# A fused state-space and channel-mix layer: another order in the first and last stages, and products on TensorE that nothing reads

## The reference

```python
def ssm(x):                                   # on the layer norm of x_in, per sequence
    x, z = split(x @ W_in)                    # 256 | 256
    dt, B, C = split(x @ W_x)                 # 256 | 16 | 16
    delta = softplus(dt @ W_dt + b_dt)
    dA = exp(delta * A)                       # 256 x 16 states per token
    h = dA * h_before + (delta * x) * B       # along the 2048 tokens
    y = sum over the 16 states of h * C  + x * D_param
    res = (y * silu(z)) @ W_out + its input
    return layernorm(res) * ln_g + ln_b
x = x_in + ssm(layernorm(x_in))
def ffn(x):                                   # on the layer norm of x
    xr, xk = mixes of x and the token before it (mu_r, mu_k)
    return sigmoid(xr @ W_r.T) * (relu(xk @ W_k.T)**2 @ W_v.T)
out = x + ffn(layernorm(x))
```

## Time and profile before

| | us |
|---|---|
| median of 3 runs | 1011.47 |
| lowest and highest | 1010.65, 1012.99 |
| the profiled execution's own time | 1010.73 |
| its span, from first to last instruction | 1008.9 |
| busy: GpSimd, PE, DVE, ACT | 931.1, 927.5, 918.1, 913.4 |
| mean granted TensorE clock | 0.978 |

### The profile page before, as it was taken

One profiled execution on the slowest core, in us unless ns is written; L12 is line 12 of the kernel. 1 busy time (PEld: TensorE's weight loads), 2 busy tenths in 40 slices (PEclk: granted clock), 3 DMA queues, 4 the chain that ended last, 5 costly groups with the idle time before them and its releaser, 6 DMA issues.

```text
span 1008.9 us, 15660 instructions
## 1 busy us (share of the span) xinstructions
PE 927.5 (92%) x4988; PEld 717.8 (71%) x4988; DVE 918.1 (91%) x1004; ACT 913.4 (91%) x2151; POOL 931.1 (92%) x408
## 2 busy tenths in 40 slices
PE   6658779999999999999999999999999999999996
PEld 3336567777778677777868777786877778688784
DVE  2989999999999999999999999999999999998974
ACT  5787999999999999999999999999999999987854
POOL 0899999999999999999999999999999999999940
PEclk9779999999999999999999999999999999999998
DMA  6444454354535544553655455365445536453410
GB/s 195 175 141 165 180 209 182 144 200 171 194 143 210 208 172 166 181 186 140 211 207 175 162 191 183 134 214 204 172 166 190 194 123 221 176 188 129 155 44 21
DMA packets 51184, 171.97 MB, mean 170 GB/s; under 512 B 5408, under 2 KB 32032, under 8 KB 34720
## 3 DMA queue, kind: packets, MB, share of 16 engines
q1 hardware_dynamic: 51104, 170.99, 46.9%
HBM read 153.67 MB, written 9.44 MB: 162 GB/s over the span
## 4 chain that ended last, share of the span: by engine, by line
ACT 55%; PE 29%; DVE 7%; issue 5%; POOL 2%; DMA 0%; ACTq 0%; SPq 0%; DVEq 0%; POOLq 0%
ACT da_ps L602 17%; PE w_ps L1181 10%; PE w_ps L1188 8%; ACT h_tok L558 3%; DVE hg L947 3%; ACT h_tok L544 3%; PE y_ps L1172 3%; ACT xn_tok L544 3%; PE w_ps L1251 2%; ACT nr L571 2%; PE w_ps L1206 2%; ACT spare L550 2%; ACT xres L782 2%; ACT L746 2%; ACT L737 2%
## 5 line engine op out<-in xcount | busy, mean ns | idle before, releaser
L494 POOL TENSOR_TENSOR dbx<-u,b_ring 128x1024 f32<-128x1024 f32 x255 | 600.3, 2375 | 9.1 <-DVE u L988 8.2
L602 ACT ACTIVATE da_ps<-delta,a_neg 128x512 f32<-128x512 f32 x512 | 332.6, 682 | 23.1 <-DVE hg L947 13.9
L507 POOL TENSOR_TENSOR hg<-hg,c_ring 128x1024 f32<-128x1024 f32 x143 | 340.2, 2379 | 3.8 <-DVE hg L947 3.1
L947 DVE TENSOR_TENSOR_SCAN hg<-da_ps,carry,dbx 128x512 f32<-128x512 f32 x216 | 263.0, 1266 | 11.5 <-ACT da_ps L602 11.4
L1172 PE MATMUL y_ps<-ident,hg 128*128 128x128 f32 x2048 | 260.5, 276 | 9.5 <-POOL hg L507 7.3
L1172 PEld LDWEIGHTS y_ps<-ident,hg 128*128 128x128 f32 x2048 | 238.0, 143 | 38.7 <-issue 21.1
L947 DVE TENSOR_TENSOR_SCAN da_ps<-da_ps,carry,dbx 128x512 f32<-128x512 f32 x168 | 208.6, 1276 | 4.4 <-ACT da_ps L602 4.0
L954 DVE TENSOR_TENSOR hg<-da_ps,c_ring 128x1024 f32<-128x1024 f32 x112 | 137.2, 1225 | 12.2 <-DVE da_ps L947 0.5
L947 DVE TENSOR_TENSOR_SCAN hg<-da_ps,dbx 128x512 f32<-128x512 f32 x72 | 83.8, 1207 | 4.5 <-ACT da_ps L602 4.5
L947 DVE TENSOR_TENSOR_SCAN da_ps<-da_ps,dbx 128x512 f32<-128x512 f32 x56 | 66.6, 1216 | 6.6 <-ACT da_ps L602 5.5
L1181 PE MATMUL w_ps<-xT,w_dtx 128*128 128x512 f32 x120 | 60.0, 623 | 7.2 <-ACT zs L617 6.4
(11 more groups left out here) (199 smaller groups left out, 1502.5 us busy)
## 6 DMA issues: line engine op xcount, KB each, us to landing
b_ring<-bc_rows_dram SPq DMA_DIRECT2D x64, 1024.0 KB, 6.6
c_ring<-bc_rows_dram SPq DMA_DIRECT2D x64, 1024.0 KB, 4.9
xres<-in_L_attn_x_in_dram SPq DMA_DIRECT2D x16, 512.0 KB, 4.7
x_tok<-in_L_attn_x_in_dram SPq DMA_DIRECT2D x15, 512.0 KB, 5.9
res<-xn_tok SPq DMA_DIRECT2D x15, 512.0 KB, 6.7
out_dram<-r_out SPq DMA_DIRECT2D x15, 512.0 KB, 3.2
bc_rows_dram<-bc_rows SPq DMA_DIRECT2D x16, 64.0 KB, 1.6
x_tok<-in_L_attn_x_in_dram SPq DMA_DIRECT2D x2, 256.0 KB, 4.1
```

The lines of the kernel that those rows point to most:

```text
L494: pool.tensor_tensor(dbx[:, n % X_RING, :, :], u[:, ip, :, :], b.to_broadcast([P, KH, LC]), ALU.mult).then_inc(s["dbx_done"], 1)
L507: pool.tensor_tensor(part, part, c_of(n).to_broadcast([P, KH, LC]), ALU.mult).then_inc(s["g_pool"], 1)
L602: act.activation(da_of(n, h), delta[:, ip, h, :], ACT.Exp, scale=a_neg[:, h, n:n + 1]).then_inc(s["da_ready"], 1)
L947: dve.tensor_tensor_scan(out, da_of(n, h), dbx[:, n % X_RING, h, :], 0.0 if first else carry[:, n, h:h + 1], ALU.mult, ALU.add).then_inc(s ...
```

## The change

The column split gets a form in which each chunk may have its own (`SPLITS`, `LAST_SPLIT`). Chunks 0 to 14 keep the old one. In chunk 15, column 12 is multiplied by C on GpSimd and no longer on DVE. The tables of step -1 and step 15 and the bank table of step 15 are all new; of them two lines are shown. The middle's tables stay. The close is reordered on PE, ACT, DVE and GpSimd; the last output half goes out as two blocks of 128 tokens, each with its own store; its second block's v product goes to a bank of its own. `keep_busy` issues products of the identity with part of w_in into a work bank; no engine reads them: four before step 0, two before the turn of h's first half and one after it.

```diff
-SPLIT = [3, 5, 6, 8, 11, 12, 14]
+SPLITS = [[3, 5, 6, 8, 11, 12, 14], [3, 5, 6, 8, 11, 12, 14]]
+LAST_SPLIT = [3, 5, 6, 8, 11, 14]
...
-VEC_HEAD = dict(small=4, sp0=4, sp1=6, u0=7, u1=9, center=11, ffn=13)
+VEC_HEAD = dict(small=6, center=6, ffn=9, sp0=10, sp1=12, u0=12, u1=15)
...
-VEC_TAIL = dict(mix0=0, mix1=0, gate=2, x20=6, x21=6, v0=8, v1=8, late_mix0=10, late_mix1=10, late_v0=14, late_v1=14)
+VEC_TAIL = dict(mix0=1, mix1=1, gate=3, x20=6, x21=6, v0=7, v1=8, late_mix0=9, late_mix1=9, late_v0=14, late_v1=14)
...
+        def split_of(i):
+            return LAST_SPLIT if i == LAST else SPLITS[i % 2]
...
             def close():
-                for v in range(2):
-                    sp.wait_ge(last_out[v], 1)
-                    sp.dma_start(out_v[LAST][:, 2 * v:2 * v + 2, :], r_out[:, 2 * v:2 * v + 2, :]).then_inc(s["out_stored"], 16)
+                sp.wait_ge(last_out[0], 1)
+                sp.dma_start(out_v[LAST][:, 0:2, :], r_out[:, 0:2, :]).then_inc(s["out_stored"], 16)
+                for j in range(2):
+                    sp.wait_ge(last_out[1], j + 1)
+                    sp.dma_start(out_v[LAST][:, 2 + j, :], r_out[:, 2 + j, :]).then_inc(s["out_stored"], 16)
...
             def close():
 
+                pool.wait_ge(s["xres_loaded"], 16 * NT)
+                part = xres[:, LAST % 2, :, :]
+                pool.tensor_tensor(part, part, b_all[:, :].unsqueeze(1).to_broadcast([P, TB, D]), ALU.add).then_inc(s["xb_done"], 1)
                 pool.wait_ge(c_loaded[GROUPS - 1], 16 * NT)
                 pool.wait_ge(s["scan_done"], KH * NS * NT - 1)
                 part = hg[:, (NS - 1) % H_RING, 0:1, :]
                 pool.tensor_tensor(part, part, c_of(NS - 1), ALU.mult).then_inc(s["g_pool"], 1)
-                pool.wait_ge(s["xres_loaded"], 16 * NT)
-                part = xres[:, LAST % 2, :, :]
-                pool.tensor_tensor(part, part, b_all[:, :].unsqueeze(1).to_broadcast([P, TB, D]), ALU.add).then_inc(s["xb_done"], 1)
...
-                    act.wait_ge(s["start_read"], read_before(NS - 1))
+                    act.wait_ge(s["start_read"], read_before(NS - 1 + h))
...
                 norm3(0)
+                share(0, xk, omk, 0)
                 norm3(1)
-                share(0)
-                share(1)
+                share(0, xr, omr, 1)
                 act.wait_ge(s["w_r_turned"], 1)
                 act.activation(w_r_last, w_r_bank, ACT.Copy).then_inc(s["w_r_set"], 1)
                 relu(0)
+                share(1, xk, omk, 0)
+                share(1, xr, omr, 1)
                 act.wait_ge(s["out_stored"], 16 * (NT - 1))
                 tanh(0)
...
                 gate(1)
+                affine_last(0)
                 second(0)
                 mean_of(0)
+                affine_last(1)
+                norm(0)
                 second(1)
-                norm(0)
                 mean_of(1)
+                mix(0, xk, muk, 1)
                 norm(1)
-                mix(0)
-                mix(1)
-                out_of(0)
-                out_of(1)
+                mix(0, h_of, mur, 2)
+                mix(1, xk, muk, 1)
+                mix(1, h_of, mur, 2)
+                out_of(0, by_block(V_LAST[0]), slice(0, 2), 1)
+                out_of(1, v_block(1, 0), 2, 1)
+                out_of(1, v_block(1, 1), 3, 2)
...
+            def keep_busy(bank, n):
+
+                for _ in range(n):
+                    pe.matmul(bank[:, :], ident[:, :], w_in[:, 0, :], start=True, stop=True)
...
                 if t == 0:
                     pe.wait_ge(s["start_read"], len(PRE))
                     pe.wait_ge(s["ffn_ev"], 3)
+                    keep_busy(work[0], 4)
...
-                need(pe, s["g_vec"], len(SPLIT) * NT)
+                pe.wait_ge(s["scan_done"], KH * (NS * NT - 1))
+                need(pe, s["g_vec"], splits(LAST, NS - 1))
                 residual(0)
                 add_up(LAST, NS - 1)
                 gated_turned(0)
                 gated_turned(1)
                 need_all_read(pe, LAST, list(TAIL_BANK))
+                wo(0)
                 residual(1)
-                wo(0)
                 wo(1)
-                h_turned(0)
                 pe.wait_ge(s["w_r_loaded"], 16)
...
                 last.then_inc(s["w_r_turned"], 1)
+                keep_busy(work[1], 2)
+                h_turned(0)
+                keep_busy(work[1], 1)
+                k_of(0)
                 h_turned(1)
-                k_of(0)
-                k_of(1)
                 pe.wait_ge(s["w_r_set"], 1)
                 r_of(0)
+                v_of(0)
+                k_of(1)
                 r_of(1)
-                v_of(0)
                 v_of(1)
```

136 lines of the change are left out of this document (77 added, 59 removed).

## The result

The changed kernel took **1003.64 us** (median of 4 runs, 1002.44 to 1004.49), the kernel before 1011.06 beside it: ratio 0.9926, 95% interval 0.9912 to 0.9939. It is 7.4 us faster; 1003.5 had been predicted. The ratios leave out one run in a slower state of the chip (old_last_step_tables, 1099.18 us at a mean granted clock of 0.841).

A forecast was written before the change was run, and what follows sets the result against it. No slack in the middle, where GpSimd is busy throughout; only ramp, last step and close can give time. Terms -2.1 - 1.3 - 4.25 = -7.65 took the profiled 1010.73 to 1003.1, 1003.8 as median; stated 1003.5 us, own range 1001.5 to 1006.

The forecast's parts named there:

- Head: Ramp before step 0: new DVE and PE order plus four unread products save 2.1 us, bounds 0 to -2.96.
- the waits on the scan, the carry and u: GpSimd's idle waits in the ramp, 0.89, 0.73 and 1.34 us, 2.96 in all, were to go.
- The rival "more than expected": After GpSimd's piece at 145.05, PE also gets full clock: up to 3 us more, 1000.5 us; chance 0.06.
- The case that the products run at a falling clock: Ramp: the four products take 6.8 us at half clock, delaying step 0's transposes some 3 us, unseen by GpSimd at first.
- The rival that the head gives nothing: Ramp: GpSimd begins 0.85 us later and still waits for chunk 1's u; 1005.6 us, chance 0.17.
- Last step: Step 15: column 15 starts at 976.0 instead of 977.31, saving 1.3 us; bounds -2.1 to +1.5.
- PE is the cap: Last step: PE's work after 955.19 stays 21.7 us, so PE is late next and limits the gain.
- GpSimd's earlier addition: Last step: adding b before the half product frees DVE's half product, about 0.7 us instead of 2.78.
- The rival that late exponentials starve DVE: Last step: late exponentials delay scans, about 2.4 us per column; four columns cost 9.5, time 1013 us; chance 0.06.
- Close: After the last step: first k product -2.85, PE stream -0.7, last output -0.7, together -4.25 us; bounds -2 to -5.2.
- PE's stream: Close, from the first k product: 11.8 us partly at half clock becomes 11.1 at full clock, -0.7 us.
- The rival that the clock falls all the same: Close: PE's clock falls despite the unread products, close gains only 2.3 us, time 1005.4 us; chance 0.10.

The follow-up runs named there:

- old_last_step_tables: Changed kernel with step 15's tables, banks and split columns as before (column 12 multiplied by DVE); 1004.36 us, ratio 0.9938 to the kernel before.
- gap_filled: Changed kernel plus 2 unread products in step 15, meant for PE's 1.97 us gap but landing behind it; 1003.98 us, ratio 0.9923.
- before_with_close_products: Kernel before plus four unread products in the old close, after the second wo product in PE's 4.76 us idle stretch; 1012.76 us, ratio 1.0012.

## Why the prediction was right, point by point

**Head, -2.1 predicted; -1.9 to -2.5 measured where PE takes over from GpSimd, -1.9 to -2.8 at the mark.** The mechanism held: the waits on the scan, the carry and u went, against a first dbx that comes later. From the first dbx to PE's start near 148 it is 118.3 us in all eight profiles with the new head and 121.1 to 121.5 in the three with the old one and no products in it; PE starts there at 149.81, 150.43 and 150.42 with the old head and at 147.93 on the mean with the new. The marks of step 2 are 166.79, 166.19 and 167.06 against 164.25. They hold a share of the clock as well, which the head's order does not set: in all fourteen profiles the clock is at half for a while behind PE's wait near 148. From PE's start to the mark it is 15.7 to 16.2 us where the mean clock of the next 8 us is 0.79 to 0.81, and 16.5 to 17.0 where it is 0.63 to 0.68, and both come with either kernel. The rival "more than expected", full clock from 145.05 on, therefore fell, and 0.95 of the 2.76 us of the first pair of profiles were luck. The first c product came at 41.41 without idle, the scans at 32.04 (41.0 and 31.5 predicted). One step of the argument was wrong: the four products and the full clock were said to be what makes u of chunk 1 ready. The clock made no difference; u is in time by the order alone. The case that the products run at a falling clock was priced for the new order, where it did not come; in the old order it cost 2.4 us, by way of the carries. The rival that the head gives nothing fell.

**Last step, -1.3 predicted; -0.93 without and +0.75 with the fall of the clock.** PE is the cap, as said, and gap_filled shows it to 0.01 us. The size came out smaller, and its parts differ: 0.5 is idle time that the new tables took from PE; the other 0.4, which the run with the old tables keeps, goes by its place with DVE's half product, for which PE had waited 0.24; the remaining 0.17 are not traced. That half product was 0.69 and ready in time, as predicted; but the reason given, GpSimd's earlier addition, was not needed in this order, since DVE came first anyway. What was missing altogether was the clock: the gap of 1.97 us at the start of step 15 is in the kernel before as well (1.96, where the clock stayed up), and the half clock behind it was not among the terms. It is worth 1.7 us; two of eight runs of the changed kernel stand in its group by their times. The rival that late exponentials starve DVE did half of what it said: GpSimd waited 2.08 us at 950.80 for DVE's hg, and DVE 1.52 at 958.20 for an exponential. But PE was the bound, and it cost nothing.

**Close, -4.25 predicted; -4.25 measured** in the profile, and -4.7 by undoing it. That it fits to the hundredth is luck. By the prediction's own terms the profiles have -2.6 to the first k product (-2.85 predicted), -0.8 for PE's stream (-0.7) and -0.5 for DVE's steps behind it (-0.7), -3.9 in all; the last 0.3 lie behind DVE's last step, where 2.5 us became 2.2 and the sum had counted nothing. By cause, the clock is 2.7 and the order with the halved output 1.6 to 2.0. The prediction put the clock's part into several terms (the turns, "-0.7" for the stream) and did not name its size. The rival that the clock falls all the same fell: col 15 to the end is 27.3 us in all ten profiles with the changed close. before_with_close_products shows that the danger was real, since four such products in another order left the fall and made the kernel slower. The skill's rule that it cited, that matmuls stay in program order (the Trainium skill, "TensorE: Matmul & The Clock Gate", step ① of Part 2), agrees with the 1.73 us of gap_filled.

**The sum.** -7.65 was predicted; the profile has -2.8 + 0.75 - 4.25 = -6.3, in an execution with the fall, and would have -8.0 without. The medians lie between, at -7.4, since two of those four runs stand in the upper group by their times. The forecast of 1003.5 came close partly because errors of both signs met: a last step 0.4 too good, a head 0.7 too poor at the mark (where the clock gave 0.95), and a fall of the clock in step 15 of which nothing was said.

**Open.** What decides whether the clock falls behind the gap in step 15, and when it comes back behind the wait near 148. In step 15, PE is busy for the whole of the 11 us ahead of the gap in both kinds of profile, and the gap is the same to 0.01 us. The kernel that would have filled the gap missed it, so whether filling it keeps all runs in the lower group wasn't tried.

## What to carry to other kernels

Cut the span at marks that both kernels have, and sum by stretch, before reading a single wait: here one stretch had lost 0.75 us that the total hid, and one had won 0.95 that was not the change's. A second profile of the same kernel tells which is which. Work that nothing reads paid here where it kept the clock up to the start of dense work; ask what stands behind it in the queue, and what PE does between it and the products it is meant for. Where an engine has no idle time left, any product added to it comes out at the end in full.

## What the runs showed of the hardware that I had not expected

- The granted clock fell behind an idle gap of 1.96 to 1.97 us on PE in some executions and not in others, of the same kernel: 106.53 and 104.82 us of last step. Runs in two groups 1.7 us apart fit this, and a median over few runs falls on either.
- Behind an idle wait of about 4 us on PE, near 148 us, the clock was at half in all fourteen profiles, but for how long differed: from there to step 2's mark it took 16.03 us in one profile of the changed kernel (mean clock 0.80 over the first 8 us) and 16.92 in the other (0.63).
- Four unread products in PE's idle stretch held the clock at 1.00 through a short turn and two idle gaps (1.32 and 1.19 us), up to about 991.2 us. Then it fell all the same, just ahead of the dense work: k products 6.45 us against 4.91 without them.
- Which of GpSimd and DVE waits for the other is decided by a tenth of a microsecond: 0.14 us ahead, GpSimd made DVE's 0.69 us product last 2.78; 0.09 us behind, its own addition went from 2.37 to 2.82.
